# A scratch buffer laid out by chunk, and the last step's output norm moved off GpSimd

## The chip, the cores and the metric

The kernel runs on one core of a Trainium2 chip. The metric is the device time of one execution in microseconds. PE is TensorE (PEld its weight loads), DVE is VectorE, ACT is ScalarE, POOL is GpSimd, and SP is SyncE, which here only issues DMA transfers.

## What is computed

```python
def _gated_delta_rule(q, k, v, g, beta):
    ...
    def step(S, inp):
        q_t, k_t, v_t, g_t, b_t = inp
        S = S * jnp.exp(g_t)[..., None, None]
        mem = jnp.einsum('bhk,bhkv->bhv', k_t, S)
        delta = (v_t - mem) * b_t[..., None]
        S = S + jnp.einsum('bhk,bhv->bhkv', k_t, delta)
        o_t = jnp.einsum('bhk,bhkv->bhv', q_t, S)
        return (S, o_t)
...
o = _gated_delta_rule(q, k, v, g, beta)
o = o * jax.lax.rsqrt(jnp.mean(o * o, axis=-1, keepdims=True) + eps)
o = o * jax.nn.silu(g_out.reshape(Bm, Tm, H, DV))
attn = o.reshape(Bm, Tm, VAL_DIM) @ o_w.T
...
xn = _layernorm(x, axis=-1)
x = x + attn(xn) + ffn(xn)
```

x is (2, 4096, 512) in float32. The attention half has 16 heads with keys of 16 and values of 32; q, k and v come from a projection, a causal convolution of 4 taps and a SiLU. The feed-forward half has 1408 hidden columns with 4-bit weights and a final root-mean-square norm.

## The kernel before, in words

**Tiles.** The sequence is cut into 32 tiles of 128 positions, both batches (NB = 2) at once. The recurrence is done by chunks of 32 positions (CH = 32, NC = 4 chunks in a tile). Within a chunk it needs the inverse of a 32x32 unit triangular matrix for each batch, chunk and head: 2 x 4 x 16 = 128 matrices, one for each partition. GpSimd solves for them in `solve` (lines 478 to 499): 31 rounds of a product (line 495) and a subtraction (line 499), with matrix (b, c, h) in partition (b, c, h) and its 1024 elements in columns 1024 to 2048 of the tile `arena` (called `lt`).

**The turn through memory.** TensorE wants the same matrices the other way: row j of every head's matrix in partition c x 32 + j (the view `tT`, in columns 0 to 1024 of `arena`). SyncE does that with two kinds of transfer, at the end of its step. When the solve has signalled `t_done`, line 406 writes all 128 partitions, 4 KB each, to the scratch `scr_t`; line 408 waits until that has landed; line 412 then reads it back in eight transfers, one for each batch and chunk, each of 32 partitions x 16 heads x 128 bytes. On TensorE `t_times_r` (lines 1190 to 1205) waits for all eight, for the keys (`rk_done`) and for `out_done`, and then runs 256 small products (line 1202) in four groups. The other scratch, `scr_a`, does the opposite turn before the solve (lines 388 and 394).

**Order of the work.** Each engine runs its own hand-written step for a pair (t, n): the second half of tile t (recurrence, norm, output projection) beside the first half of tile n = t + 1 and n's feed-forward. `run` calls it once for the first tile, 30 times in a hardware loop, once for the last pair, and once with n absent: the last step, which has only the recurrence and the output of tile 31. On TensorE a step begins with `project(0)`, 16 products for the gates, `project(1)` to `project(4)`, and then `t_times_r(0)`, `project(5)`, `t_times_r(1)`, `t_times_r(2)`, `turn_qk(0)` and so on. Waits are in program order: whatever stands behind `t_times_r(0)` on TensorE waits with it. SyncE's next instructions after the reads are the loads of the next tile's x (line 384).

**The output norm.** In the last step, as in every step with a t, the output o is copied out of PSUM and squared by ScalarE (lines 754 and 759) and summed over each head's 32 values by VectorE (line 1032). GpSimd (`gated_and_scaled`, lines 513 to 527) multiplies o by the gate (line 517), forms mean plus eps (line 519), takes the power -0.5 (line 522) and scales o (line 527), for each batch. TensorE then turns o (`turn_o`, line 1347), ScalarE copies it (`o_columns`, line 667), TensorE multiplies by `wo` (line 1357), VectorE adds it to the result (line 912) and SyncE stores it (line 399).

**Other waits on the write.** `t_written` is also waited for by `solve` of the next tile (line 481) and by VectorE's `keep_rows(0)` (line 921), which overwrites the columns that the write reads.

Of the kernel before, what the change touches and what calls it, by code (L numbers as in the profile page):

```python
# [18 lines left out]
F32 = mybir.dt.float32  # L19
# [5 lines left out]
ALU = mybir.AluOpType  # L25
# [3 lines left out]
P = 128  # L29
NB = 2  # L30
# [61 lines left out]
def build(nc, A, out):  # L92
    NIT = A["x"].shape[1] // P
    scr_a = nc.dram_tensor("scr_a", (NB, NC, CH, H, CH), F32).ap()
    scr_t = nc.dram_tensor("scr_t", (NB, NC, H, CH, CH), F32).ap()

    with ExitStack() as ctx:
# [30 lines left out]
        negA = sb("negA", [P, H])  # L128
        eps = sb("eps", [P, 1])
        mhalf = sb("mhalf", [P, NB, H])  # L130

# [71 lines left out]
        a_read = signal("a_read", 128)  # L203
        t_written = signal("t_written", 16)
        t_read = signal("t_read", 128)

# [172 lines left out]
        def sp_step(eng, t, n, more):  # L379
            if more:  # L380
                m = n.next()
                hold(eng, *x_turned.at(n, NB))
                for b in range(NB):
                    eng.dma_start(xt[:, b, :], A["x"][b, bass.ds(m.number * P, P), :]).then_inc(x_loaded.sem, 16)
            if n:
                for b in range(NB):
                    hold(eng, *a_done.at(n, b + 1))
                    eng.dma_start(scr_a[b].rearrange("c j h i -> (c j) (h i)"), kbq[:, b, :]).then_inc(a_written.sem, 16)
                    hold(eng, *a_written.at(n, 16 * (b + 1)))
                    if b == 0:  # L390
                        hold(eng, *gram_out.at(n, NB))
                    for c in range(NC):
                        p0 = (b * NC + c) * H
                        eng.dma_start(la[p0:p0 + H, :, :],
                                      scr_a[b, c].rearrange("j h i -> h j i")).then_inc(a_read.sem, 16)
            if t:
                for b in range(NB):
                    hold(eng, *attn_added.at(t, b + 1))
                    eng.dma_start(out[b, bass.ds(t.number * P, P), :], obuf[:, b, :]).then_inc(out_stored.sem, 16)
                hold(eng, *out_stored.at(t, 16 * NB))  # L400
            if not n:
                return
            for b in range(NB):
                eng.dma_start(obuf[:, b, :], A["x"][b, bass.ds(n.number * P, P), :]).then_inc(res_loaded.sem, 16)
            hold(eng, *t_done.at(n, 1))
            eng.dma_start(scr_t[:, :, :, :, :].rearrange("b c h j i -> (b c h) (j i)"),
                          arena[:, 1024:2048]).then_inc(t_written.sem, 16)
            hold(eng, *t_written.at(n, 16))
            for b in range(NB):
                for c in range(NC):  # L410
                    s = slice(c * CH, (c + 1) * CH)
                    eng.dma_start(tT[s, b, :, :], scr_t[b, c].rearrange("h j i -> j h i")).then_inc(t_read.sem, 16)

# [64 lines left out]
        def solve(eng, n):  # L478

            if not n.first:  # L480
                hold(eng, *t_written.at(n.before(), 16))
            hold(eng, *qk_done.at(n, NB))
# [46 lines left out]
        def pool_step(eng, t, n, more):  # L529
            if n:  # L530
# [7 lines left out]
                keys_for_state(eng, t, n)  # L538
            if t:
                gated_and_scaled(eng, t)  # L540
# [28 lines left out]
        def act_step(eng, t, n, more):  # L569
# [92 lines left out]
            def o_columns():  # L662
                if not t:
                    return
                for b in range(NB):
                    eng.wait_ge(*o_turned.at(t, b + 1))
                    eng.activation(oT[b].rearrange("p k t -> p (k t)"), PS[:, 6 + b, :],
                                   ACT.Copy).then_inc(ot_copied.sem, 1)

            def y_rows():  # L670
                if not t:
# [65 lines left out]
            u_rows(1)  # L737
            decay(1)
            u_rows(2)
            masked_keys(0)  # L740
# [19 lines left out]
            unit(3)  # L760
            eng.preload_act_table_set(SILU)
            if n:
                gate(0)
                eng.wait_ge(*taps_done.at(n, NQKV))
# [8 lines left out]
                gate(2)  # L773
            if not n:
                o_columns()
                return
# [23 lines left out]
        def _(eng):  # L800
# [8 lines left out]
            eng.preload_act_table_set(EXP)  # L809
            eng.wait_ge(zeroed.sem, 4)  # L810
            first = Tile(0, 0, first=True)
# [36 lines left out]
        def dve_step(eng, t, n, more):  # L848
# [65 lines left out]
            def keep_rows(b):  # L914
# [5 lines left out]
                if t and b == 0:  # L920
                    eng.wait_ge(*t_written.at(t, 16))
                eng.tensor_copy(qk_rows[:, b, :], PS[:, 6 + b, :]).then_inc(qk_kept.sem, 1)
# [114 lines left out]
            hidden(1)  # L1037
            if not n:
                result(0)
                result(1)  # L1040
                return
# [16 lines left out]
        def _(eng):  # L1058
            eng.memset(eps[:, :], 1e-6).then_inc(zeroed.sem, 1)
            eng.memset(mhalf[:, :, :], -0.5).then_inc(zeroed.sem, 1)  # L1060
            eng.memset(halo[:, :, :, :], 0.0).then_inc(zeroed.sem, 1)
            eng.memset(S[:, :, :, :, :], 0.0).then_inc(zeroed.sem, 1)
            first = Tile(0, 0, first=True)
# [31 lines left out]
        def pe_step(eng, t, n, more):  # L1095
# [94 lines left out]
            def t_times_r(q):  # L1190
                if not t:
                    return
                if q == 0:
                    hold(eng, *rk_done.at(t, NB))
                    hold(eng, *t_read.at(t, 16 * NB * NC))
                    hold(eng, *out_done.at(t, NB))
# [274 lines left out]
        def _(eng):  # L1471
            eng.wait_ge(first_loaded.sem, 16 * 2)
            eng.wait_ge(zeroed.sem, 4)
            transpose_x(eng, Tile(0, 0, first=True), None)
# [66 lines left out]
```

## Time and profile before

| | before |
|---|---|
| median of 3 runs | 3350.01 us (3347.69 to 3350.68) |
| time of the profiled execution | 3347.2 us |
| its span | 3345.4 us |
| mean granted clock of TensorE | 0.988 of full speed |
| PE busy | 3174.2 us (95%) |
| DVE busy | 2429.0 us (73%) |
| POOL busy | 1840.9 us (55%) |
| ACT busy | 1664.4 us (50%) |

The span goes from the first to the last record of the profiled execution; the execution's own time is 1.8 us longer. An engine's busy time counts instructions, not the waits between them. A DMA's row in a timeline is the time in which SP issues it, not the time in which the data moves; that is seen in the DMA share (mean busy share of the core's 16 DMA engines) and GB/s of a window. Idle time in square brackets stands before a row, with what ended it.

### The profile page before, as it was taken

The numbers are of one execution on the slowest core, as the hardware profiler recorded it, in microseconds if no ns is written. First come the engines' busy times: TensorE is split into PE (matmuls) and PEld (weight loads), VectorE is DVE, ScalarE is ACT, GpSimd is POOL, SyncE is SP. The second block draws the span as 40 slices with busy tenths as digits, with TensorE's granted clock in tenths as the row PEclk, the third lists the DMA queues.
The fourth block names the chain that finished last, engine by engine and source line by source line (L and its number), as shares of the span: only waits on it lengthen the run. The fifth ranks groups of instructions, "written<-read, shape, count | busy, mean of one in ns | idle before, by whom it ended". The sixth has DMA issues, their size and how long they took to land.

```text
span 3345.4 us, 118358 instructions
## 1 busy us (share of the span) xinstructions
PE 3174.2 (95%) x45632; PEld 2253.2 (67%) x45632; DVE 2429.0 (73%) x5407; ACT 1664.4 (50%) x3306; POOL 1840.9 (55%) x2737
## 2 busy tenths in 40 slices
PE   5999999999999999999999999999999999999995
PEld 4666766766666766666666667666667666666664
DVE  7677777777777777777777777777777777777772
ACT  3444554545554445545445545445545455544452
POOL 3565455665455664456654456654556654466543
PEclk8999999999999999999999999999999999999996
DMA  3111111111111111111111111111111111111111
GB/s 111 39 46 27 37 43 33 45 39 27 40 40 39 46 33 30 43 34 45 46 27 37 43 33 46 45 26 35 43 36 46 36 28 43 37 42 46 27 31 30
DMA packets 318316, 132.07 MB, mean 39 GB/s; under 512 B 277088, under 2 KB 278880, under 8 KB 317792
## 3 DMA queue, kind: packets, MB, share of 16 engines
q1 hardware_dynamic: 313824, 119.26, 14.2%
q8 instruction: 383, 6.28, 0.8%
q10 hardware_dynamic: 4096, 6.42, 0.6%
q14 instruction: 13, 0.11, 0.0%
HBM read 75.30 MB, written 50.33 MB: 38 GB/s over the span
## 4 chain that ended last, share of the span: by engine, by line
PE 63%; DVE 13%; POOL 8%; issue 8%; ACT 4%; DMA 2%; SPq 1%; ACTq 1%; DVEq 1%; POOLq 0%
PE PS L1148 14%; PE PS L1216 7%; PE PS L1135 7%; PE PS L1104 6%; PE PS L1136 6%; PE PS L1357 5%; DVE arena L876 4%; POOL arena L499 4%; POOL work L495 3%; PE PS L1281 3%; PE PS L1202 3%; DVE inner L978 2%; PE PS L1234 2%; DVE arena L373 2%; PE PS L1252 2%
## 5 line engine op out<-in xcount | busy, mean ns | idle before, releaser
L876 DVE SCALAR_TENSOR_TENSOR arena<-PS,sc,arena 128x256 f32<-128x256 f32 x2112 | 1004.3, 482 | 294.0 <-ACT arena L596 193.6
L1135 PE MATMUL PS<-xh,wgu 128*128 128x256 f32 x2816 | 871.5, 341 | 36.0 <-DVE arena L876 35.5
L596 ACT ACTIVATE arena<-PS,sc 128x256 f32<-128x256 f32 x704 | 330.7, 475 | 759.6 <-PE PS L1136 703.6
L1136 PE MATMUL PS<-xl,wgu 128*128 128x256 f32 x2816 | 698.8, 281 | 0.0
L1148 PE MATMUL PS<-wdn,inner 128*128 128x512 f32 x1408 | 650.7, 592 | 0.0
L1135 PEld LDWEIGHTS PS<-xh,wgu 128*128 128x128 f32 x2816 | 531.2, 189 | 156.1 <-issue 85.2
L495 POOL TENSOR_TENSOR work<-arena 128x31 f32<-128x31 f32 (+15 forms) x992 | 511.4, 516 | 138.4 <-DMA arena<-scr_a 63.2
L499 POOL TENSOR_TENSOR arena<-arena,work 128x31 f32<-128x31 f32 (+15 forms) x992 | 543.7, 548 | 77.8
L1136 PEld LDWEIGHTS PS<-xl,wgu 128*128 128x128 f32 x2816 | 530.3, 188 | 83.2 <-issue 83.2
L1104 PE MATMUL PS<-xnT,wqkv 128*128 128x256 f32 x2048 | 498.7, 392 | 27.4 <-ACT inner L576 19.6
L1104 PEld LDWEIGHTS PS<-xnT,wqkv 128*128 128x128 f32 x2048 | 384.5, 194 | 107.5 <-ACT inner L576 33.2
L860 DVE SCALAR_TENSOR_TENSOR qkv<-inner,cw,qkv 128x256 f32<-128x256 f32 x768 | 419.6, 583 | 19.8 <-ACT qkv L583 10.6
L1148 PEld LDWEIGHTS PS<-wdn,inner 128*128 128x128 f32 x1408 | 245.6, 189 | 199.8 <-issue 199.3
L373 POOL TENSOR_TENSOR R<-arena,ckg 128x256 f32<-128x256 f32 x64 | 57.2, 912 | 399.9 <-DVE ckt L942 399.9
L1216 PE MATMUL PS<-wg,xnT 128*128 128x512 f32 x512 | 263.4, 618 | 0.1
L1357 PE MATMUL PS<-wo,arena 128*128 128x512 f32 x512 | 241.2, 594 | 0.0
L615 ACT ACTIVATE ub<-PS 32x512 f32<-32x512 f32 x256 | 136.8, 580 | 198.1 <-PE PS L1234 194.6
L517 POOL TENSOR_TENSOR arena<-arena 128x512 f32<-128x512 f32 x64 | 80.5, 1280 | 272.5 <-ACT qkv L759 272.5
L898 DVE TENSOR_TENSOR tmp<-PS,bdmask 128x128 f32<-128x128 f32 x256 | 74.2, 290 | 209.5 <-PE PS L1252 205.1
L888 DVE TENSOR_TENSOR inner<-arena,sg 128x256 f32<-128x256 f32 x352 | 203.6, 586 | 30.1
L607 ACT ACTIVATE sg<-arena 128x256 f32<-128x256 f32 x352 | 145.2, 412 | 153.9 <-DVE arena L876 153.5
L1054 DVE SCALAR_TENSOR_TENSOR obuf<-PS,yr,obuf 128x512 f32<-128x512 f32 x64 | 45.1, 746 | 217.8 <-POOL yr L511 217.8
(141 smaller groups left out, 4553.8 us busy)
## 6 DMA issues: line engine op xcount, KB each, us to landing
xt<-in_x SPq DMA_DIRECT2D x64, 256.0 KB, 2.8
scr_a<-arena SPq DMA_DIRECT2D x64, 256.0 KB, 2.4
arena<-scr_a SPq DMA_DIRECT2D x256, 64.0 KB, 3.2
obuf<-in_x SPq DMA_DIRECT2D x64, 256.0 KB, 2.8
scr_t<-arena SPq DMA_DIRECT2D x32, 512.0 KB, 2.7
arena<-scr_t SPq DMA_DIRECT2D x256, 64.0 KB, 2.3
out<-obuf SPq DMA_DIRECT2D x64, 256.0 KB, 2.0
wqkv<-in_wqkv ACTq DMA_DIRECT2D x1, 2048.0 KB, 12.9
```

The costliest lines, as they stand in the source:

```text
L495: eng.tensor_tensor(pr, la[:, j, j + 1:].unsqueeze(1).broadcast_to([P, w, r]), bc(lt[:, 0:w, j], r), ALU.mult).then_inc(solve_part.sem, 1)
L499: eng.tensor_tensor(tail, tail, pr, ALU.subtract).then_inc((t_done if j == CH - 2 else solve_part).sem, 1)
L596: eng.activation(fa[:, u % 4, :], PS[:, bank(u, 0), 0:NB * P], ACT.Copy, scale=sc[:, u % 2, KB * m:KB * m + 1]).then_inc(fa_scaled.sem, 1)
L860: eng.scalar_tensor_tensor(out=acc, in0=cin[:, mm, :, k:k + P], scalar=cw[:, mm, k:k + 1], in1=acc, op0=ALU.mult, op1=ALU.add).then_inc((t ...
L876: eng.scalar_tensor_tensor(out=fa[:, u % 4, :], in0=PS[:, bank(u, k // 2), k % 2 * NB * P:][:, 0:NB * P], scalar=sc[:, u % 2, KB * m + k:K ...
L888: eng.tensor_tensor(inner[:, m, :], fa[:, (2 * m + 1) % 4, :], sg[:, m % 2, :], ALU.mult).then_inc(h_done.sem, 1)
L1104: ins = eng.matmul(PS[:, proj_bank(m), 0:NB * P], wqkv[:, kb, m * P:(m + 1) * P], xnT[:, kb, :], start=(kb == 0), stop=(kb == KB - 1))
L1135: eng.matmul(o, w, xh[:, k, :], start=True, stop=False)
L1136: ins = eng.matmul(o, w, xl[:, k, :], start=False, stop=True)
L1148: ins = eng.matmul(PS[:, b, :], inner[:, m, b * P:(b + 1) * P], wdn[:, m, :], start=(m == 0), stop=(m == FM - 1))
L1216: ins = eng.matmul(PS[:, 4 + b, :], xnT[:, kb, b * P:(b + 1) * P], wg[:, kb, :], start=(kb == 0), stop=(kb == KB - 1))
L1357: ins = eng.matmul(PS[:, 6 + b, :], oT[b][:, kb, :], wo[:, kb, :], start=(kb == 0), stop=(kb == KB - 1))
```

## The change

There are two parts. The scratch `scr_t` is laid out with the chunk outermost, so that for one chunk both batches lie together. The write becomes two transfers, one for each batch, each from 64 partitions to 4 chunks x 16 heads; the read becomes four transfers, one for each chunk, each of 32 partitions x 32 (batch, head) x 128 bytes. The bytes are the same. The counts that others wait for follow.

In the last step alone, GpSimd no longer gates and scales the output: VectorE multiplies by the gate and by the scale, and ScalarE makes the scale as exp(-0.5 ln(mean + eps)) in `last_roots`, with a table load between the two. The load of the logarithm's table stands earlier in that step, between `u_rows(1)` and `u_rows(2)`, and the load of the SiLU table is left out there. The new eps tile is set once at the start, by one more memset that TensorE and ScalarE wait for with the others.

```diff
-    scr_t = nc.dram_tensor("scr_t", (NB, NC, H, CH, CH), F32).ap()
+    scr_t = nc.dram_tensor("scr_t", (NC, NB, H, CH, CH), F32).ap()
...
-        t_written = signal("t_written", 16)
-        t_read = signal("t_read", 128)
+        t_written = signal("t_written", 32)
+        t_read = signal("t_read", 64)
...
             hold(eng, *t_done.at(n, 1))
-            eng.dma_start(scr_t[:, :, :, :, :].rearrange("b c h j i -> (b c h) (j i)"),
-                          arena[:, 1024:2048]).then_inc(t_written.sem, 16)
-            hold(eng, *t_written.at(n, 16))
             for b in range(NB):
-                for c in range(NC):
-                    s = slice(c * CH, (c + 1) * CH)
-                    eng.dma_start(tT[s, b, :, :], scr_t[b, c].rearrange("h j i -> j h i")).then_inc(t_read.sem, 16)
+                eng.dma_start(scr_t[:, b].rearrange("c h j i -> c h (j i)"),
+                              arena[b * NC * H:(b + 1) * NC * H, 1024:2048]).then_inc(t_written.sem, 16)
+            hold(eng, *t_written.at(n, 16 * NB))
+            for c in range(NC):
+                s = slice(c * CH, (c + 1) * CH)
+                eng.dma_start(tT[s, :, :, :].rearrange("j b h i -> j (b h) i"),
+                              scr_t[c].rearrange("b h j i -> j (b h) i")).then_inc(t_read.sem, 16)
...
                 keys_for_state(eng, t, n)
-            if t:
+            if t and n:
                 gated_and_scaled(eng, t)
...
+            def last_roots():
+
+                eng.wait_ge(*so_done.at(t, NB))
+                eng.activation(ro[:, :, :], so[:, :, :], ACT.Ln, scale=1.0 / DV, bias=epso[:, :]).then_inc(ro_done.sem, 1)
+                eng.preload_act_table_set(EXP)
+                eng.wait_ge(*ro_done.at(t, 1))
+                eng.activation(ro[:, :, :], ro[:, :, :], ACT.Exp, scale=-0.5).then_inc(ro_done.sem, 1)
...
             decay(1)
+            if not n:
+                eng.preload_act_table_set(LOG)
             u_rows(2)
...
             unit(3)
-            eng.preload_act_table_set(SILU)
             if n:
+                eng.preload_act_table_set(SILU)
...
             if not n:
+                last_roots()
                 o_columns()
...
             if not n:
+                for b in range(NB):
+                    eng.wait_ge(*gs_done.at(t, 1))
+                    eng.tensor_tensor(sq[:, b, :], sq[:, b, :], gs[:, b, :], ALU.mult).then_inc(o_gated.sem, 1)
+                for b in range(NB):
+                    eng.wait_ge(*ro_done.at(t, 2))
+                    eng.wait_ge(*o_gated.at(t, b + 1))
+                    oh = sq[:, b, :].rearrange("p (h v) -> p h v", v=DV)
+                    eng.tensor_tensor(oh, oh, bc(ro[:, b, :], DV), ALU.mult).then_inc(o_scaled.sem, 1)
                 result(0)
                 result(1)
                 return
...
-                    hold(eng, *t_read.at(t, 16 * NB * NC))
+                    hold(eng, *t_read.at(t, 16 * NC))
```

## Rows read from the trace of the kernel before

**Rows 1.** The profile's page: busy time of the engines, and the chain that ended last.

```profile
PE 3174.2 (95%) x45632; PEld 2253.2 (67%) x45632; DVE 2429.0 (73%) x5407; ACT 1664.4 (50%) x3306; POOL 1840.9 (55%) x2737
...
PE 63%; DVE 13%; POOL 8%; issue 8%; ACT 4%; DMA 2%; SPq 1%; ACTq 1%; DVEq 1%; POOLq 0%
```

**Rows 2.** All matrix products on the triangles (line 1202): count, first and last start; transfer waits.

```profile
L1202 PE MATMUL PS<-R,arena x8192: 201/201/283, 145.4 to 3293.6; 32*32 32x48 f32 x200
...
  DMA arena<-scr_t: 9.8, 1
```

**Rows 3.** Timeline of SP's queue at one tile boundary: start us, us, engine, line.

```profile
1657.16 0.33 SPq L406 DMA_DIRECT2D scr_t<-arena  x1
1659.91 4.05 SPq L412 DMA_DIRECT2D arena<-scr_t  x8
```

**Rows 4.** The same boundary in windows: last columns PE's clock, DMA share, GB/s.

```profile
1657.98:1658.50 0.52, 0.52 (x6) 0.47 (x4) 0.00 (x0) 0.52 (x1) 0.41 (x1) 1.00 1.06 433
1658.50:1659.00 0.50, 0.50 (x8) 0.50 (x6) 0.10 (x1) 0.49 (x2) 0.48 (x2) 1.00 0.96 393
1659.00:1659.42 0.42, 0.42 (x6) 0.42 (x5) 0.42 (x1) 0.22 (x1) 0.42 (x1) 1.00 0.61 244
...
1661.50:1662.50 1.00, 1.00 (x6) 0.89 (x5) 1.00 (x2) 0.04 (x1) 0.88 (x1) 1.00 0.71 112
1662.50:1663.50 1.00, 1.00 (x6) 0.88 (x5) 0.92 (x4) 0.97 (x3) 0.00 (x0) 1.00 0.84 131
```

**Rows 5.** Timeline of PE at the same boundary.

```profile
1667.60 0.88 PE L1202 MATMUL PS<-R,arena 32*32 32x48 f32 x64
```

**Rows 6.** SP's queue, the next tile boundary.

```profile
1758.94 0.33 SPq L406 DMA_DIRECT2D scr_t<-arena  x1
```

**Rows 7.** Timeline of PE there.

```profile
1768.94 0.88 PE L1202 MATMUL PS<-R,arena 32*32 32x48 f32 x64
```

**Rows 8.** One tile's period in one window.

```profile
1667.60:1768.94 101.34, 98.43 (x1427) 69.92 (x1427) 74.59 (x170) 51.53 (x104) 57.04 (x86) 1.00 0.15 37
```

**Rows 9.** SP's queue in the last two steps.

```profile
3279.51 0.33 SPq L406 DMA_DIRECT2D scr_t<-arena  x1
3282.24 4.05 SPq L412 DMA_DIRECT2D arena<-scr_t  x8
```

**Rows 10.** Timeline of PE there.

```profile
3288.27 4.50 PE L1202 MATMUL PS<-R,arena 32*32 32x48 f32 x240 [9.79 <-DMA arena<-scr_t]
```

**Rows 11.** SP's queue: four reads of the other scratch, scr_a.

```profile
1614.23 1.90 SPq L394 DMA_DIRECT2D arena<-scr_a  x4
```

**Rows 12.** Windows from 1.7 us after these four reads began to be issued.

```profile
1615.91:1616.91 1.00, 1.00 (x4) 0.46 (x3) 0.90 (x3) 0.00 (x0) 1.00 (x1) 1.00 0.79 127
...
1618.41:1618.91 0.50, 0.50 (x7) 0.50 (x7) 0.47 (x2) 0.33 (x1) 0.00 (x0) 1.00 0.04 5
```

**Rows 13.** The last step's end: POOL.

```profile
3322.42 2.48 POOL L517 TENSOR_TENSOR arena<-arena 128x512 f32<-128x512 f32 x2 [41.82 <-ACT qkv L759]
...
3325.39 5.42 POOL L522 TENSOR_TENSOR ro<-ro,mhalf 128x32 f32<-128x32 f32 x1 [0.18 <-POOL ro L519]
3330.89 2.05 POOL L527 TENSOR_TENSOR arena<-arena,ro 128x512 f32<-128x512 f32 x2
```

**Rows 14.** The last step's end: DVE.

```profile
3322.44 1.28 DVE L1032 TENSOR_REDUCE so<-qkv 128x16 f32<-128x512 f32 x2 [7.31 <-ACT qkv L759]
3338.82 0.69 DVE L912 TENSOR_TENSOR obuf<-obuf,PS 128x512 f32<-128x512 f32 x1 [15.10 <-PE PS L1357]
```

**Rows 15.** The last step's end: ACT.

```profile
3322.88 1.28 ACT L761 ACT_TABLE_LOAD   x1
```

**Rows 16.** The last step's end: PE.

```profile
3331.99 2.12 PE L1347 MATMUL PS<-ident,arena 128*128 128x128 f32 x8 [11.30 <-POOL arena L527]
```

**Rows 17.** ACT in a middle tile: a logarithm of 128x32.

```profile
1666.08 0.21 ACT L705 ACTIVATE lnz<-ee 128x32 f32<-128x32 f32 x1
```

**Rows 18.** ACT in the last step, where the new table load is put.

```profile
3306.99 1.07 ACT L615 ACTIVATE ub<-PS 32x512 f32<-32x512 f32 x2 [3.42 <-PE PS L1234]
```

More of the change, by code:

```diff
@@ L129, in build @@
         eps = sb("eps", [P, 1])
+        epso = sb("epso", [P, 1])
         mhalf = sb("mhalf", [P, NB, H])
@@ L480, in solve @@
             if not n.first:
-                hold(eng, *t_written.at(n.before(), 16))
+                hold(eng, *t_written.at(n.before(), 16 * NB))
             hold(eng, *qk_done.at(n, NB))
@@ L809, in _ @@
             eng.preload_act_table_set(EXP)
-            eng.wait_ge(zeroed.sem, 4)
+            eng.wait_ge(zeroed.sem, 5)
             first = Tile(0, 0, first=True)
@@ L920, in keep_rows @@
                 if t and b == 0:
-                    eng.wait_ge(*t_written.at(t, 16))
+                    eng.wait_ge(*t_written.at(t, 16 * NB))
                 eng.tensor_copy(qk_rows[:, b, :], PS[:, 6 + b, :]).then_inc(qk_kept.sem, 1)
@@ L1061, in _ @@
             eng.memset(halo[:, :, :, :], 0.0).then_inc(zeroed.sem, 1)
+            eng.memset(epso[:, :], float(np.finfo(np.float32).eps)).then_inc(zeroed.sem, 1)
             eng.memset(S[:, :, :, :, :], 0.0).then_inc(zeroed.sem, 1)
@@ L1472, in _ @@
             eng.wait_ge(first_loaded.sem, 16 * 2)
-            eng.wait_ge(zeroed.sem, 4)
+            eng.wait_ge(zeroed.sem, 5)
             transpose_x(eng, Tile(0, 0, first=True), None)
```

## Prediction

> **What bounds the kernel.** I read the page first. TensorE is busy 95% of the span, and the chain that ended last runs on it for 63%, with VectorE and GpSimd far behind [rows 1]. So a stall that holds TensorE's queue in every tile costs its whole length, and a saving on a DMA queue is worth something only where TensorE waits for it. Next come the instructions that use what the changed transfers bring. The products on the triangles run from 145.4 to 3293.6 us, and only one of their 32 visits waits for the reads, for 9.8 us: the last [rows 2]. In the other 31 the turn through memory is hidden.
>
> How well it is hidden decides this case. At a middle boundary the write is issued at 1657.16 and the first read at 1659.91, 2.75 us later [rows 3]; TensorE comes to the products at 1667.60, or 10.44 us after the write was issued [rows 5]. One tile later the same distance is 1768.94 - 1758.94 = 10.00 us [rows 6, 7]. I take the mean, 10.2 us, as the time that the turn may take. What it does take is seen where nothing else is in the way, in the last step: write at 3279.51, reads from 3282.24, TensorE at 3288.27 [rows 9, 10]. That is 2.73 + 6.03 = 8.76 us. The cover is thus 10.2 - 8.8 = 1.4 us. Anything that makes the turn longer by more than 1.4 us is paid once a tile, and anything that makes it shorter is paid back once, in the last step.
>
> **The write.** In the trace the write's data are three windows: 0.52 x 433 + 0.50 x 393 + 0.42 x 244 = 524 KB [rows 4]. At a DMA share of 0.96 they move 393 GB/s, so 16 engines fully used move some 409 GB/s and the data need 1.28 us. The rest of the 2.75 us, 1.47 us, is issue, start and landing. The new write is two transfers whose destination leads with 4 chunks, each of 16 rows; the old one led with 128 rows. The trace has no transfer that leads with fewer than 16 rows, so it does not show how many engines share such a one. I bound it from both sides. If all 16 share it, the data still need 1.28 us, and the second issue (0.33 us, like the first [rows 3]) is hidden behind the first one's data: plus 0.0 to 0.4 us. If the leading rows are what is dealt out, 4 engines get everything, at 409 / 4 = 102 GB/s: 524 / 102 = 5.13 us, or plus 3.85 us. Both writes would go to the same 4, since the second is dealt out like the first. Fewer than 4 is not plausible, as 4 leading rows and 64 partitions both divide by 4. I take the long end: the leading dimension is the one that both sides of every transfer in this kernel could always be dealt by, and 4 is all that it now has. From write to first read: 1.47 + 5.13 = 6.60 us.
>
> The Trainium skill states a rule for this, in "DMA: Bandwidth & Descriptors", section "Why a DMA increments its semaphore by 16 and not by 1": a transfer uses the largest count of engines, up to 16, that divides the slowest dimension of both its sides. By it the count here is 4, and the sum would be the one below. No row of this trace shows it.
>
> **The reads.** Eight issues take 4.05 us [rows 3, 9]; four would take some 2.0 us. If the reads went at the pace at which they are issued, 2.0 us would be saved. But the data move at 112 to 131 GB/s with a DMA share of 0.71 to 0.84 [rows 4], and the packets stay 128 bytes: 524 KB at 121 GB/s are 4.3 us, longer than the issues of even the old form. So the pace is mostly that of the packets. Were the share to rise from 0.78 to 1, the same packets would need 3.4 us and 0.9 us would be saved. The other side is the reads of the other scratch. Four issued in 1.90 us [rows 11], with the same small packets, still move data in the window that ends 4.7 us after their first issue, at a share of 0.04, while up to 2.7 us it was 0.79 [rows 12]: once the issues run ahead, a few engines straggle. 4 x 64 KB at 121 GB/s are 2.2 us of data, so the stragglers stretch a batch by some 1.5 us (an estimate, from 4.7 less 2.2 and less about 1 us of start). Between a gain of 2.0 and a loss of 1.5 us I take a gain of 0.3 us, near the data rate of the row.
>
> The Trainium skill's "DMA: Bandwidth & Descriptors", section "Rules for kernel authors", advises to coalesce small transfers, since under 64 KB one pays mostly overhead. The old reads are 64 KB each. By that rule alone the gain would be near the 2.0 us of the issues; the data rate in the rows speaks against it.
>
> **The sum for a middle tile.** New turn: 6.60 + 6.03 - 0.3 = 12.3 us, against 10.2 us at which TensorE arrives: it stalls 2.1 us. Behind the wait in its queue stand project(5), the other product groups, turn_qk and all of the recurrence; ScalarE and VectorE wait for these in turn, so nothing downstream goes on without them. In a whole tile of 101.34 us TensorE is idle for 2.9 us [rows 8], in short pieces, so there is little to swallow a stall. GpSimd's next solve starts from what TensorE makes later, so it shifts by the same amount and the next boundary looks alike. The first boundary has more cover: its products start at 145.4 [rows 2]. That leaves 30 tiles: 30 x 2.1 = +63 us. The x loads behind the reads on SP are issued some 2 us later, and their data are used over 10 us later: nothing. The later `t_written` waits of VectorE and GpSimd are passed well before they are reached: nothing.
>
> **The last step.** The turn is uncovered: 12.3 - 8.8 = +3.6 us. Then the norm. Before, GpSimd gates from 3322.42 for 2.48 us, takes the power from 3325.39 for 5.42 us, and scales from 3330.89; TensorE starts at 3331.99 [rows 13, 16]. After: the sums start at 3322.44, 0.64 us each [rows 14], done by about 3323.8. ScalarE's logarithm takes 0.21 us [rows 17], the table load 1.28 us [rows 15], the exponential 0.21 us as its like, and the handovers some 0.4 us: 3325.9. VectorE's scaling of one batch I price at 0.65 us, by the addition of the same size that takes 0.69 us [rows 14]; its two gatings (1.3 us) fit between 3323.8 and 3325.9. TensorE starts at about 3326.5: -5.5 us. The logarithm's table is loaded in a wait of 3.42 us [rows 18], so it costs nothing; without that cover it would cost 1.28 us. The extra memset is one small instruction before the input has landed: nothing. Last step: 3.6 - 5.5 = -1.9 us.
>
> **Total.** The profiled execution's own 3347.2 + 63 - 1.9 = 3408.3 us; its time stands 2.8 us below the median of the runs. I predict 3408 us.
>
> **Rivals.**
> (A, forecast, 0.74) Four engines; a stall of 1.4 to 3.2 us a tile. Its own range is 3386 to 3442 us.
> (B, 0.13) All 16 engines share the writes. The turn then takes at most 8.8 + 0.4 us, below 10.2; nothing in the loop changes, and the norm alone pays. 3350 - 5.5 - 0.3 = 3344 us. For it: every transfer in the trace reaches a share near 1 or is bound by packets. Against: none leads with so few rows. It decides as soon as the write's data need less than 1.28 + 1.4 = 2.7 us. This is the one that ends on the faster side.
> (C, 0.07) Four engines, but the reads are bound by their issues: a gain of 1.0 to 2.0 us, and a stall of 0.4 to 1.4 us. 3347 + 12 to 42 + up to 2 - 5.5: 3355 to 3385 us.
> (D, 0.06) Four engines, and the reads straggle as scr_a's do, 1.5 us later than before: a stall of 2.1 + 0.3 + 1.5 = 3.9 us. 3347 + 117 + 5.4 - 5.5 = 3464 us.
>
> **Range and chances.** 3352 to 3442 us holds A and C and leaves out B and D, some 2 in 10. About 0.2% (6.7 us) is what a measurement of this kernel can tell from no change. Below 3343.3 us lies about half of B: 0.06. Within 0.2% the rest of B and a little of C: 0.09. Slower: 0.85.
>
> **What would show it.** In the trace after: the distance from the first write to the first read (6.6 us by A, 2.8 to 3.2 us by B); the DMA share while the write runs (near 0.25 over 5 us, or near 1 over 1.3 us); the time from first read to last landing; the products on the triangles waiting for a DMA in some 30 tiles, about 2 us each; the distance from write to products (12.3 us); and in the last step TensorE's turn_o some 5.5 us earlier behind the squares. I am wrong if the write's windows show a share near 1, or if the waits are there and the tile's period is not longer than 101.3 us.

## The result, and the profile after

The changed kernel takes 3588.34 us (median of 4 runs, 3587.82 to 3590.29) against 3350.35 us, a ratio of 1.071 (95% interval 1.070 to 1.073). Slower was forecast; the size was not: 3408 us, range 3352 to 3442. The profiled span grew by 243.0 us, from 3345.4 to 3588.4 us. Where a kernel ran more than once, its time and ratio here and below are of its fast runs; an execution in a slower state, as one of e1_rows64 at 4911.6 us, is left out.

On the page, the shares of busy time and the chain that ended last answer to [rows 1]:

```profile
PE 3239.1 (90%) x45632; PEld 2302.4 (64%) x45632; DVE 2419.8 (67%) x5412; ACT 1668.3 (46%) x3309; POOL 1836.7 (51%) x2731
...
PE 31%; POOL 30%; DMA 19%; issue 6%; DVE 6%; SPq 5%; POOLq 2%; ACT 1%; ACTq 0%; DVEq 0%
POOL arena L501 15%; POOL work L497 14%; DMA scr_t<-arena 8%; PE PS L1238 7%; PE PS L1126 6%; DMA scr_a<-arena 4%; DMA arena<-scr_t 4%; PE PS L1224 3%; DMA arena<-scr_a 3%; PE PS L1303 3%; SPq L395 3%; PE PS L1256 2%; PE PS L1274 2%; DVE arena L374 1%; SPq L413 1%
```

TensorE's share of the chain fell from 63% to 31%. GpSimd's solve (line 501 is 499 of before, and line 497 is 495), DMA and the scratch buffers took its place: the turn through memory has become part of the loop that sets the time. In the waits (who waited, on what, us in total, times, longest), TensorE's products on the triangles, line 1224 now, wait for the reads on all 32 visits, where before only the last one did [rows 2]:

```profile
PE PS L1224 <- DMA arena<-scr_t: 192.1, 32, 16.8
```

One boundary shows where this comes from. SP's queue and TensorE, as in [rows 3, 5]:

```profile
1772.42 1.14 SPq L408 DMA_DIRECT2D scr_t<-arena  x2
1782.37 2.15 SPq L413 DMA_DIRECT2D arena<-scr_t  x4
```

```profile
1788.35 1.50 PE L1224 MATMUL PS<-R,arena 32*32 32x48 f32 x64 [5.37 <-DMA arena<-scr_t]
1789.78 3.78 PE L1126 MATMUL PS<-xnT,wqkv 128*128 128x256 f32 x8
...
1795.03 0.66 PE L1182 MATMUL PS<-ident,qkv 128*128 128x128 f32 x4
```

First read 9.95 us after the first write (before 2.75, forecast 6.60). TensorE is at the products 15.93 us after the write (before 10.44 and 10.00, forecast 12.3); from first read to products it takes 5.98 us (forecast 5.73). The first product after the stall and project(5) behind it are slow as well: 3.78 us for eight products that took 1.99 us in other places. The windows tell both (columns: window, length, busy time of PE, PEld, DVE, ACT and POOL with counts, TensorE's clock, DMA share, GB/s):

```profile
1774.00:1776.00 2.00, 2.00 (x17) 1.95 (x17) 1.80 (x3) 0.50 (x2) 1.80 (x3) 1.00 0.23 43
1776.00:1778.00 2.00, 2.00 (x11) 1.77 (x10) 1.97 (x3) 0.24 (x1) 1.68 (x1) 1.00 0.25 70
1778.00:1780.00 2.00, 2.00 (x11) 1.74 (x11) 1.60 (x5) 1.95 (x5) 0.00 (x0) 1.00 0.24 94
1780.00:1782.00 2.00, 1.80 (x9) 1.27 (x8) 1.78 (x8) 1.92 (x6) 0.00 (x0) 1.00 0.11 43
...
1788.35:1790.35 2.00, 2.00 (x65) 1.81 (x66) 0.00 (x0) 0.00 (x0) 0.00 (x0) 0.50 0.08 24
1794.00:1796.00 2.00, 2.00 (x144) 1.77 (x135) 0.00 (x0) 0.79 (x2) 0.00 (x0) 1.00 0.04 8
```

While the writes run, the DMA share is 0.23 to 0.25: four engines of sixteen. But they move 43, then 70, then 94 GB/s, and not the 102 GB/s that four should. They do not end together either: from 1780 to 1782 the share is 0.11, on average fewer than two engines, and the reads wait for the last of them. And when TensorE starts again after 5.4 us of idling, its granted clock is 0.5 (1.2 GHz) and comes back to 1.0 by 1794.

The period of the loop, from the first writes' first and last starts. The instructions of the tile `scr_t` (duration min, median, max, first and last start):

```profile
L408 SPq DMA_DIRECT2D scr_t<-arena x64: 507/523/666, 133.2 to 3521.9; - x64
```

The last step's first write is at 3521.36, so a tile takes (3521.36 - 133.2) / 31 = 109.3 us, against (3279.51 - 133.2) / 31 = 101.5 us before: +7.8 us, 242 of the 243 us. One tile in one window, here from one first write to the next:

```profile
1772.42:1882.19 109.77, 101.26 (x1430) 71.93 (x1429) 74.59 (x168) 52.09 (x106) 57.10 (x85) 0.97 0.15 35
```

The rest is the last step, +7.0 us in the turn and -5.6 us in the norm. The turn, as [rows 9, 10]: 3537.09 - 3521.36 = 15.73 us, against 8.76.

```profile
3521.36 1.09 SPq L408 DMA_DIRECT2D scr_t<-arena  x2
3531.18 2.21 SPq L413 DMA_DIRECT2D arena<-scr_t  x4
```

```profile
3537.09 4.68 PE L1224 MATMUL PS<-R,arena 32*32 32x48 f32 x240 [16.82 <-DMA arena<-scr_t]
```

The norm, as [rows 13 to 16], on ScalarE, VectorE and TensorE:

```profile
3573.08 0.32 ACT L675 ACTIVATE ro<-so,epso 128x32 f32<-128x32 f32 x1 [0.90 <-DVE so L1045]
3573.42 1.28 ACT L676 ACT_TABLE_LOAD   x1
3574.71 0.23 ACT L678 ACTIVATE ro<-ro 128x32 f32<-128x32 f32 x1
```

```profile
3571.77 1.28 DVE L1045 TENSOR_REDUCE so<-qkv 128x16 f32<-128x512 f32 x2 [7.60 <-ACT qkv L771]
...
3574.97 1.29 DVE L1059 TENSOR_TENSOR arena<-arena,ro 128x512 f32<-128x512 f32 x2 [0.73 <-ACT ro L678]
```

```profile
3575.72 1.97 PE L1369 MATMUL PS<-ident,arena 128*128 128x128 f32 x8 [5.70 <-DVE arena L1059]
```

From the first sum to TensorE's turn_o it is 3575.72 - 3571.77 = 3.95 us, against 3331.99 - 3322.44 = 9.55 us: 5.6 us less.

### The profile page after: what moved, and what is told of

Read it like the earlier page. It is cut to its first block, busy times and chain, and to the rows that moved or that the text cites. A ratio compares the mean times of both kernels' runs of the same rounds, so it can differ in the third digit from the quotient of the medians.

```text
span 3588.4 us, 118230 instructions
## 1 busy us (share of the span) xinstructions
PE 3239.1 (90%) x45632; PEld 2302.4 (64%) x45632; DVE 2419.8 (67%) x5412; ACT 1668.3 (46%) x3309; POOL 1836.7 (51%) x2731
## 4 chain that ended last, share of the span: by engine, by line
PE 31%; POOL 30%; DMA 19%; issue 6%; DVE 6%; SPq 5%; POOLq 2%; ACT 1%; ACTq 0%; DVEq 0%
POOL arena L501 15%; POOL work L497 14%; DMA scr_t<-arena 8%; PE PS L1238 7%; PE PS L1126 6%; DMA scr_a<-arena 4%; DMA arena<-scr_t 4%; PE PS L1224 3%; DMA arena<-scr_a 3%; PE PS L1303 3%; SPq L395 3%; PE PS L1256 2%; PE PS L1274 2%; DVE arena L374 1%; SPq L413 1%
## 5 line engine op out<-in xcount | busy, mean ns | idle before, releaser
L1126 PE MATMUL PS<-xnT,wqkv 128*128 128x256 f32 x2048 | 546.4, 420 | 27.6 <-ACT inner L578 19.2
L1126 PEld LDWEIGHTS PS<-xnT,wqkv 128*128 128x128 f32 x2048 | 416.0, 210 | 120.0 <-ACT inner L578 32.2
L1224 PE MATMUL PS<-R,arena 32*32 32x48 f32 x8192 | 129.2, 224 | 192.8 <-DMA arena<-scr_t 192.1
L1224 PEld LDWEIGHTS PS<-R,arena 32*32 32x32 f32 x8192 | 115.7, 122 | 226.5 <-issue 226.5
L935 DVE COPY arena<-PS 128x512 f32<-128x512 f32 x64 | 44.0, 687 | 309.6 <-ACT arena L635 300.0
```

Of the source, the lines that this page charges most:

```text
L1126: ins = eng.matmul(PS[:, proj_bank(m), 0:NB * P], wqkv[:, kb, m * P:(m + 1) * P], xnT[:, kb, :], start=(kb == 0), stop=(kb == KB - 1))
L1224: ins = eng.matmul(x_rows(c, r)[:, 0:3, (b * NHALF + f) * 2 + e, :], tT[s, b, h, :], R[s, b, h, :], start=(b + f + e == 0), stop=False, sk ...
```

## The experiments

Line numbers are those of each kernel. "First read" is the time from the first write's issue to the first read's, "products" that from the first write's issue to TensorE's start on them, both at a boundary in the middle. All use the changed kernel as the base unless something else is said. In the second column [4 x 16] stands for 4 leading rows of 16 each; the count of engines is read from the DMA share. One packet of a write is one row of 4 KB; at the rate of the write before (409 GB/s on 16 engines) an engine needs 0.16 us for it. What the runs on the write gave:

| run | what it writes | engines | first read, us | time, us | ratio to before |
|---|---|---|---|---|---|
| before | 1 x 128 rows | 16 | 2.75 | | 1 |
| changed | 2 x [4 x 16] | 4 | 9.95 | 3588.3 | 1.071 |
| e1_rows64 | 2 x 64 | 16 | 3.85 | 3338.5 | 0.998 (0.997 to 0.999) |
| e3_lead8 | 2 x [8 x 8] | 8 | 5.74 | 3368.4 | 1.008 (1.006 to 1.009) |
| e2_pad | 2 x [4 x 16], 132 KB apart | 4 | 10.04 | 3577.0 | 1.069 (1.067 to 1.070) |
| e12_onelead4 | 1 x [4 x 32] | 4 | 10.19 | 3593.0 | 1.074 (1.072 to 1.076) |
| e6_serial | 2 x [4 x 16], one at a time | 4 | 11.16 | 3605.5 | one run |
| e14_rows | 2 x [4 x 16], side by side | 4 | 9.94 | 3574.8 | one run |
| e13_alt4 | 2 x [4 x 16], even and odd partitions | 4 | 8.49 | 3523.0 | one run |
| e15_quarters | 4 x [4 x 8] | 4 | 7.24 | 3454.4 | one run |

**e1_rows64: the same two writes and four reads, but 64 rows lead.** The scratch's rows are ordered chunk, head, batch, so that a batch's 64 rows have one stride.

```diff
-scr_t (NC, NB, H, CH, CH);  write scr_t[:, b] "c h j i -> c h (j i)"
+scr_t (NC, H, NB, CH, CH);  write scr_t[:, :, b] "c h j i -> (c h) (j i)"
-tT = arena[:, 0:1024] "p (b h i) -> p b h i"
+tT = arena[:, 0:1024] "p (h b i) -> p b h i"
```

> The changed kernel, but each of the two writes leads with 64 rows (rows of the scratch ordered chunk, head, batch), and the four reads stay. Theory 1 (the leading dimension of a transfer sets how many engines share it): first read some 2.9 us after the first write instead of 9.95, a turn of 8.9 us, hidden again below the 10.2 us of cover; the loop is as before and the last step keeps its gain: about 3345 us. Theory 2 (two writes and four reads of twice the size are slow by themselves, whatever leads): near the 3588 us of the changed kernel.

SP's queue in it:

```profile
1656.61 1.12 SPq L408 DMA_DIRECT2D scr_t<-arena  x2
1660.46 2.44 SPq L413 DMA_DIRECT2D arena<-scr_t  x4
```

3338.5 us, ratio 0.998 (0.997 to 0.999), and 3.85 us to the first read instead of 2.9. Theory 1 holds: with two writes and four reads as in the changed kernel the whole of the 238 us is gone, so what leads in the write made it slower.

**e3_lead8: eight leading rows.** Rows in the order chunk, half, batch, eight heads.

```diff
+scr_t (NC * 2, NB, H // 2, CH, CH);  write scr_t[:, b] "c h j i -> c h (j i)"
+tT = arena[:, 0:1024] "p (e b g i) -> p b e g i"
```

> The changed kernel, with writes that lead with 8 (chunk and half of the heads) x 8 rows; same four reads. If the leading dimension sets the engines, 8 sem packets a write, and a DMA share of 0.5 at most. Theory B of e2 with time going as one over the engines: data 4.15 us, first read after 5.8 us, turn 11.8 us, a stall of 1.6 us without a fall of TensorE's clock: 3345 + 48 + 3 = 3396 us. With the old packet rate on 8 engines, 2.6 us of data, turn 10.2 us: 3345 to 3350 us. If the count of engines is not the cause: 3588 us.

```profile
1665.90 1.27 SPq L408 DMA_DIRECT2D scr_t<-arena  x2
1671.64 2.30 SPq L413 DMA_DIRECT2D arena<-scr_t  x4
```

```profile
1668.90:1669.90 1.00, 1.00 (x7) 0.90 (x7) 1.00 (x2) 0.00 (x0) 1.00 (x1) 1.00 0.49 156
```

1.008 (1.006 to 1.009), with a stall of 1 us a tile (41.5 us in 31 waits, 12.4 of them in the last step); the first read comes where theory B put it (5.8 us), the time below its 3396 us. With 64, 8 and 4 leading rows the first read comes after 3.85, 5.74 and 9.95 us. Less the 1.47 us of issue and landing these are 2.4, 4.3 and 8.5 us, close to one over the number of engines (38, 34 and 34 when multiplied by it). With the share, 0.49 here for eight engines and 0.23 to 0.25 for four, that settles the count. What it leaves open is the rate: at 0.16 us a packet, the 128 packets need 20 us summed over the engines and not 34.

**e2_pad: four engines, 132 KB apart in memory.**

```diff
+scr_t (NC, NB * H + 1, CH, CH);  write scr_t[:, b*H:(b+1)*H]; read scr_t[c, 0:NB*H]
```

> The changed kernel, with one unused row behind each chunk in the scratch, so that the four leading rows of a write lie 132 KB apart and not 128 KB. The writes still lead with 4. Theory A (addresses 128 KB apart get in each other's way and make the write take 8.3 us of data where four engines at the old packet rate need 5.1): first read after about 6.7 us, a turn of 12.7 us, 3345 + 30 x 2.5 + 4 = about 3424 us. Theory B (four engines are slow for another reason): as the changed kernel, 9.9 us and 3588 us.

First read after 10.04 us, ratio 1.069 (1.067 to 1.070): theory A falls.

**e4_norm: the last step's norm alone**, on the kernel before.

> The kernel before with the new last-step norm alone. The prediction's term: 5.5 us less, 3344.9 us. The rival, that the table loads or the extra wait eat it: within 2 us of the kernel before.

3337.3 us against 3344.8 of the kernel before beside it, ratio 0.998 (0.997 to 0.999). The term of 5.5 us lies in the interval (3.7 to 9.7 us less).

**e5_twice: the kernel before, with its write done twice**, to measure the cover with a known delay.

```diff
 hold(eng, *t_written.at(n, 16))
+eng.dma_start(scr_t ..., arena[:, 1024:2048]).then_inc(t_written.sem, 16)
+hold(eng, *t_written.at(n, 32))
```

> The kernel before, with the same 128-row write done a second time after the first has landed: the turn is 2.75 us longer, 11.5 us, with nothing else changed. The prediction's cover of 1.4 us (10.2 less 8.8) and one for one passing: a stall of 1.3 to 1.4 us in 30 tiles and 2.75 us in the last step, +43 us. If the stall were taken up elsewhere in the tile: below +10 us.

The write is at 1789.17 and the products here:

```profile
1800.76 0.88 PE L1205 MATMUL PS<-R,arena 32*32 32x48 f32 x64 [1.60 <-DMA arena<-scr_t]
```

```profile
PE PS L1205 <- DMA arena<-scr_t: 55.1, 31, 12.7
```

The turn is 11.6 us and the stall 1.6 us here, 55.1 us in 31 waits. Less the last step's 12.7 us, that is 1.4 us a tile, as expected. The time rose by more, to a ratio of 1.017 (1.014 to 1.019), which is +48 to +63 us: so 1.4 us of stall cost some 1.8 us. Nothing in the tile takes a stall up; it costs a little more than itself. TensorE's rows show where: behind the stall it pauses in the same products for 14.5 us in 24 pauses, waiting for nothing that the profile shows; the kernel before has 1.0 us in 3 such pauses.

**e10_warm and e11_warm12: does the clock cost the rest?** Products of a projection into a free bank ahead of the wait keep TensorE busy through the stall (20 in the first, 12 in the second).

```diff
+if n:
+    for i in range(12):
+        eng.matmul(PS[:, 7, 0:NB * P], wqkv[:, i % KB, 0:P], xnT[:, i % KB, :], start=True, stop=True)
 hold(eng, *t_read.at(t, 16 * NC))
```

> The changed kernel, with 20 products of a projection (into a free bank, their result unused) ahead of the wait for the reads, 20 x 0.24 = 4.8 us of the 5.4 to 6.0 us that TensorE stands still there. If the clock at half speed after that idle time is what costs the 2.1 us a tile beyond the stall: the clock stays at 1.0, the period falls from 109.1 to about 107 us and the time to 3588 - 30 x 2.1 = 3525 us. If the clock has no part in it: 3588 us.

It went to 3644.1 us, ratio 1.090. The expectation had the price of a product wrong, as TensorE's rows show (the write is at 1799.52):

```profile
1809.51 8.80 PE L1219 MATMUL PS<-xnT,wqkv 128*128 128x256 f32 x40
1818.24 0.88 PE L1227 MATMUL PS<-R,arena 32*32 32x48 f32 x64
```

Each product is two records, and 20 take 8.80 us, so they hold TensorE until 18.7 us after the write. It tells nothing of the clock's price.

> As e10_warm, but with 12 products in place of 20: there each took 0.44 us and not 0.24 (8.8 us for the 20), so that they themselves held TensorE until 18.7 us after the write. 12 take 5.3 us and end before the reads land at 15.9 us. The clock stays at 1.0, the period falls from 109.1 to about 107 us and the time to 3588 - 30 x 2.1 = 3525 us. If the clock has no part in it: 3588 us.

The boundary with the write at 1770.66:

```profile
1786.35 0.88 PE L1227 MATMUL PS<-R,arena 32*32 32x48 f32 x64 [0.36 <-DMA arena<-scr_t]
1787.16 1.99 PE L1126 MATMUL PS<-xnT,wqkv 128*128 128x256 f32 x8
...
1793.25 0.36 PE L1227 MATMUL PS<-R,arena 32*32 32x48 f32 x13 [1.31 <-issue]
```

The stall is 0.36 us, project(5) takes 1.99 us again and not 3.78: the clock stays up here. turn_qk(0) comes 4.2 us after the first product (1790.58 - 1786.35), against 6.7 us in the changed kernel (1795.03 - 1788.35). In the kernel before it takes 4.4 us (1672.04 - 1667.60). So the fall of the clock costs over 2 us at the boundary. The whole run's granted clock is 0.985 here and 0.960 in the changed kernel. But the time is 3573.5 us and not 3525, only 14.8 us or 0.5 us a tile less than the changed kernel: in the last group of small products TensorE now stops for 1.31 us, waiting for nothing that the profile shows ("issue"). Over the run this is 45.8 us in 43 pauses, or 1.5 us a tile, of the kind that e5_twice has too; the changed kernel, at the slower clock, has one, of 0.7 us. What they are stays open. So the clock's price is shown at the boundary and not in the total: what the kernel would gain from a clock that stays up lies between the 0.5 us a tile that e11 got and the 2.2 us of the boundary.

**e6_serial: one write at a time.**

```diff
 eng.dma_start(scr_t[:, b] ..., arena[b * NC * H:(b + 1) * NC * H, 1024:2048])
+hold(eng, *t_written.at(n, 16 * (b + 1)))
```

> The changed kernel, with a wait between its two writes, so that only one is on its way at a time. Theory C (the two writes hinder each other on the four engines): each takes 1.47 + 16 packets x 0.16 = 4.0 us, the first read comes after 8.1 us instead of 9.95, and the time falls by some 30 x 1.9 = 55 us. Theory D (a write that only four engines share is slow by itself at 4.15 us of data): first read after 11.3 us or more, and 3588 + 30 x 1.4 = about 3630 us.

```profile
1781.81 6.13 SPq L408 DMA_DIRECT2D scr_t<-arena  x2
1792.97 2.21 SPq L413 DMA_DIRECT2D arena<-scr_t  x4
```

11.16 us to the first read, so some 5.6 us for each write and 4.1 us of data (5.6 - 1.47) for 16 packets an engine: theory D, though the time rose less than it foretold (3605.5 us against about 3630). The two writes do not hinder each other.

**e12_onelead4: one write, still four engines.** The solve's matrices stand in partition order chunk, batch, head (as in e9_onewrite, below), the scratch has one unused row behind each chunk.

> As e9_onewrite (one write of all 128 partitions, four reads), but the write leads with 4 (chunks of 32 rows, one unused row behind each). It tells the count of engines from the split in two. At the packet time of the 16-engine write (0.16 us): 32 packets are 5.1 us, first read after 6.6 us, turn 12.5 us, stall 2.3 us, 3337 + 30 x 2.3 + 4 = 3410 us. At the 0.26 us a packet that the changed kernel's writes need on average: 8.3 us, first read after 9.8 us, about 3580 us.

```profile
1772.97 0.59 SPq L407 DMA_DIRECT2D scr_t<-arena  x1
1783.16 2.42 SPq L412 DMA_DIRECT2D arena<-scr_t  x4
```

10.19 us, ratio 1.074 (1.072 to 1.076): the split in two is not the cause either. e9_onewrite, below, writes the same rows of the same partitions at once and differs in the unused row alone, so that its write leads with 128 rows: 3344.7 us against 3593.0.

**e7_halves and e8_evenodd: the kernel before, its write in two, 16 engines each**, once by lower and upper half of the partitions and once by even and odd ones.

```diff
+for b in range(NB):    # e7
+    eng.dma_start(scr_t[b] "c h j i -> (c h) (j i)", arena[b * 64:(b + 1) * 64, 1024:2048])
+for b in range(NB):    # e8
+    eng.dma_start(scr_t "b c h j i -> (b c h) (j i)"[b:P:2], arena[b:P:2, 1024:2048])
```

> The kernel before, with the write split into two of 64 rows, each to one contiguous half of the scratch; 16 engines share each. e1_rows64 took 2.2 us of data for the same bytes (first read after 3.85 us) where the one write takes 1.4 (2.75 us). If its scattered rows were the cause: 1.4 us and a first read after some 3.0 us here. If it is that each transfer reads only half of the partitions: 2.2 us and 3.85 us again. The time stays with the kernel before either way, within 0.1%, since both are below the 10.2 us of cover.

> The kernel before, with the write split into two of 64 rows, one of the even and one of the odd partitions. In e7_halves, with the lower and the upper half of the partitions, the first read came after 3.83 us where the one write has 2.75. If that is because each transfer reads from one half of the partitions only: about 3.1 us here (2.75 and one more issue). If it is two transfers as such: 3.83 us again. The time stays with the kernel before.

e7, its queue and the window in which the writes' data move:

```profile
1758.70 1.12 SPq L407 DMA_DIRECT2D scr_t<-arena  x2
1762.53 4.05 SPq L413 DMA_DIRECT2D arena<-scr_t  x8
```

```profile
1759.83:1762.00 2.17, 2.17 (x19) 2.09 (x19) 1.92 (x3) 0.54 (x2) 1.98 (x3) 1.00 0.94 242
```

e8, the same:

```profile
1757.14 1.13 SPq L407 DMA_DIRECT2D scr_t<-arena  x2
1760.23 4.06 SPq L413 DMA_DIRECT2D arena<-scr_t  x8
```

```profile
1758.29:1759.73 1.44, 1.44 (x15) 1.44 (x15) 1.26 (x2) 0.48 (x2) 1.25 (x3) 1.00 0.91 361
```

The same bytes, engines and number of transfers: 242 GB/s from one half of the partitions, 361 GB/s from every second one, with the DMA share above 0.9 in both, and 3.83 against 3.09 us to the first read. In e8 the rows of each write also alternate in memory, but so do those of e1_rows64, which reads halves and has 3.85 us. So the partitions that a transfer reads set its speed here. The times: e8 3345.7 us (one run), e7 1.002 (1.001 to 1.003), which is 0.2% more than expected and not explained; none of its reads is waited for before the last step.

**e13_alt4, e14_rows: source or destination?** e13 puts batch 0 into the even and batch 1 into the odd partitions. e14 lets the four engines write side by side in memory.

```diff
-arena[b * NC * H:(b + 1) * NC * H, 1024:2048]
+arena[b:P:NB, 1024:2048]                        # e13
-scr_t (NC, NB, H, CH, CH)
+scr_t (NB, H, NC, CH, CH)                       # e14
```

> The changed kernel, with batch 0 in the even and batch 1 in the odd partitions (the reads of scr_a land there), so that each write still leads with 4 x 16 rows on four engines, but takes its rows from all 128 partitions, and each engine's 16 from 32 partitions. At 16 engines this made the split write as fast as it can be (e8_evenodd). If reading from few partitions is also what keeps the four engines at 0.26 us a packet: data 5.1 us, first read after 6.7 us, 3345 + 30 x 2.5 = about 3420 us. If not: first read after 9.9 us and 3588 us.

> The changed kernel, with the scratch's rows in the order batch, head, chunk: each write still leads with 4 chunks x 16 rows on four engines, but the four write side by side (rows 4 KB apart, each engine's next row 16 KB on) and not 128 KB apart. e2_pad moved them only to 132 KB. If where the four engines write in memory is what slows them: first read clearly before 9.9 us, down to 6.7 us. If not: 9.9 us and 3588 us; the reads, of 128 bytes every 16 KB, may change by some tenths.

e13's queue:

```profile
1743.47 1.18 SPq L408 DMA_DIRECT2D scr_t<-arena  x2
1751.96 2.32 SPq L413 DMA_DIRECT2D arena<-scr_t  x4
```

```profile
1745.47:1746.47 1.00, 1.00 (x9) 0.97 (x9) 1.00 (x3) 0.00 (x0) 0.82 (x2) 1.00 0.08 16
...
1747.47:1748.47 1.00, 1.00 (x7) 0.87 (x6) 1.00 (x2) 0.08 (x1) 0.83 (x1) 1.00 0.27 111
```

e13 takes 1.5 us off the first read, between its two forecasts; e14, at 9.94 us, nothing. Where the rows go has no part in it, where they come from has. In e13 nearly the whole loss is at the start: the third microsecond after the issue moves 16 GB/s, and from the fifth on the four engines run at the full 111 GB/s.

**e15_quarters: four engines that read elsewhere.** If the leading rows are dealt out in order, engine k reads partitions 16k to 16k + 15 of its half in the changed kernel, so that engines 0 and 2, and 1 and 3, are 32 partitions apart as long as they keep step. Here they are 8, 16 and 24 apart. (The matrices land under other heads and chunks, so this kernel does not compute the right result; its transfers are of the same sizes.)

```diff
-for b in range(NB): write scr_t[:, b] from arena[b * 64:(b + 1) * 64]
+for q in range(4):
+    h = slice(q % 2 * HG, (q % 2 + 1) * HG)
+    eng.dma_start(scr_t[:, q // 2, h] "c h j i -> c h (j i)", arena[q * 32:(q + 1) * 32, 1024:2048])
```

> The changed kernel, with the write in four transfers of 32 partitions, each leading with 4 groups of 8 rows (the matrices land in the scratch under other heads and chunks than they belong to, so the recurrence computes with misplaced triangles; the bytes, engines and packets are the same). Still four engines and 32 packets for each. What changes is which partitions the four engines read at the same time: 8 apart here, 16 apart in the changed kernel. Theory P (engines whose partitions are 32 apart share a way out of SBUF, as the halves of e7 against the even and odd rows of e8 suggest; here no two of the four are 32 apart): 32 packets at 0.16 us = 5.1 us of data, first read after 6.8 us, 3345 + 30 x 2.6 = about 3425 us. Theory Q (four engines are slow whatever they read): first read after 9.9 us or more, 3588 us or more.

```profile
1704.86 2.67 SPq L409 DMA_DIRECT2D scr_t<-arena  x4
1712.10 2.21 SPq L414 DMA_DIRECT2D arena<-scr_t  x4
```

```profile
1717.91 0.88 PE L1225 MATMUL PS<-R,arena 32*32 32x48 f32 x64 [2.35 <-DMA arena<-scr_t]
```

7.24 us to the first read, and 13.05 us to the products, with a stall of 2.35 us. The data need 7.24 - 1.47 = 5.8 us with four issues (2.67 us in all) among them, near the 5.1 us of the packets. Theory P foretold the first read within half a microsecond (6.8 us; its time, 3425 us, was 29 us short), and it accounts for 2.7 of the 3.3 us by which the forecast of the write was short. Two things keep it from being shown in full. The write is in four transfers here and not in two, and that alone was not tried (one against two makes no gain: 10.19 and 9.95 us). And e13's four engines are 32 partitions apart from one another as well, and still reach 111 GB/s once they are under way; that engines fall out of step there would explain it, but no run tested it.

The Trainium skill's "SBUF — State Buffer", section "Door 1: The DMA port swizzle (why `[64,N]` ≈ `[32,N]`)", says that bits 4 to 2 and bit 6 of a partition's number pick one of 16 ports, so that partitions 32 apart within a half share one and a half reaches only 8 ports. The traces agree in three places: the halves at 242 GB/s, the even rows at 361, and the four engines that are not 32 apart at nearly the full packet rate. By the same rule e13's engines share ports two by two as those of the changed kernel do, and there the 111 GB/s are not explained by it.

**e9_onewrite: chunk order in the partitions, one write, four reads.**

```diff
-p0 = (b * NC + c) * H
+p0 = (c * NB + b) * H
+eng.dma_start(scr_t "c b h j i -> (c b h) (j i)", arena[:, 1024:2048])
```

> The changed kernel, with the solve's matrices in partition order chunk, batch, head (the reads of scr_a land there), so that one write of 128 rows fills the scratch laid out by chunk, and the four reads stay: first read 2.75 us after the write, a turn of 2.75 + 5.9 = 8.7 us. The loop as before, the last step as in e4_norm or 0.1 us better: a ratio of 0.998 to the kernel before. If four reads of twice the size were worth the 2.0 us of their issues, the last step would begin its products 6.8 us after the write.

The last step:

```profile
3278.51 0.33 SPq L407 DMA_DIRECT2D scr_t<-arena  x1
3281.25 2.14 SPq L412 DMA_DIRECT2D arena<-scr_t  x4
```

```profile
3286.93 3.34 PE L1223 MATMUL PS<-R,arena 32*32 32x48 f32 x155 [9.55 <-DMA arena<-scr_t]
```

Ratio 1.000 (0.999 to 1.001), 3344.7 us in that comparison. The turn of the last step is 3286.93 - 3278.51 = 8.42 us, 0.3 us less than before. This is the four reads' whole worth: 3286.93 - 3281.25 = 5.68 us from first read to products, against 6.03. The loop's cover of 10.2 us hides even that. e9's last step has the same norm as e4, so a ratio like e4's 0.998 was due; the two intervals just touch, and no run sets them side by side. The versions that measured clearly below the kernel before are e4_norm (3337.3 us) and e1_rows64 (3338.5 us), by 0.2%. Both have the new norm, and it is the only part of the change with a gain that shows in the time.

## Why the prediction was wrong

**What held.** The turn was hidden by a cover of 1.4 us: e5_twice measured it. The leading dimension deals out the engines: a share of 0.25, and e1 and e3. The reads gained 0.3 us when measured alone (forecast 0.3); the rival of 2.0 us fell. TensorE swallows none of a stall. The norm: -5.6 us (forecast -5.5). The rule that the prediction cites for the count of engines agrees with the trace: a share of 0.25 with 4 leading rows, of 0.49 with 8.

**Where it failed: the write's term.** "If the leading rows are what is dealt out, 4 engines get everything, at 409 / 4 = 102 GB/s: 524 / 102 = 5.13 us." The count was right, the rate was not. The rate of a 16-engine transfer was divided by four as if each engine carried its own rate wherever it reads. It took 9.95 us to the first read in place of 6.60, +3.3 us: the data need 8.5 us and not 5.13. That this hangs on the partitions that the four engines read is shown (e13, e15; e2 and e14 rule out the place in memory); that it is engines 32 partitions apart slowing each other down is the reading that fits e15_quarters (7.24 us), e3 and e7 against e8, with e13's later stretch unexplained. And the 5.13 us stood as the upper bound: the range had nothing beyond.

**A term that was not in the sum: the clock.** The forecast's stall of 2.1 us was priced as itself. At 5.4 us and more TensorE's clock fell to 1.2 GHz in every tile, and the stretch from the first product to turn_qk(0) grew by some 2 us (6.7 us, against 4.4 before and 4.2 in e11). At the boundary shown the stall of 1.6 us in e5_twice left it at 1.0, and the run's clock is 0.988 as before. In e15_quarters, with stalls of 2.8 us a tile, it is 0.977 against 0.989: so a stall near the 2.1 us of the forecast may already bring it down in some tiles.

**The sum again.** Products at 15.9 us instead of 10.2: +5.7 us a tile. Behind them +2.1 us, the length of what the clock costs at the boundary (2.2 us over before); but e11, which kept the clock up, got back only 0.5 us of it. Together +7.8 us, as measured; times 31 is 242 us (the first boundary, whose 12.2 us of cover I had let pass, is stalled too), and the last step adds 7.0 - 5.6. The forecast's 2.1 us a tile was short by 3.3 (write), 0.3 (reads: 5.98 us from first read to products against 5.73) and 2.1 (behind the stall, where it had nothing).

**The rivals.** B (16 engines) fell; it is what e1_rows64 brings about. C and D were about the reads, and neither came. The true outcome was none of the four: the range reached only as far as the mechanisms that I had named for the reads, while the doubtful number was the write's.

## What to carry to other kernels

The DMAs here were dealt out over the engines by their slowest dimension, so ask of every rearranged transfer what now leads on each side: writing "c h (j i)" for "(c h) (j i)" cost 7% here. Fewer issues are worth little where the data rate sets the pace (0.3 us of 6.0 here), and that only where somebody waits. When a hidden transfer may come out from its cover, price the wait beyond its length too, since TensorE came back at half its clock after 5.4 us; and set the range by the least known rate, not by the best known.

## What the runs showed of the hardware

- The rate of a write depends on the partitions that its engines read at the same time. Four engines took 8.5 to 8.7 us of data for 512 KB with sources 16 or 32 apart (changed kernel, e12), 7.0 us in e13 with every second partition, and 5.8 us with sources 8 apart (first read less 1.47 us). On 16 engines, 242 GB/s from 64 neighbouring partitions and 361 GB/s from 64 even ones.
- Where the rows go in memory did not matter: 4 KB, 128 KB or 132 KB between the engines gave 9.94, 9.95 and 10.04 us to the first read.
- An issue on SP of a write that leads with 4 x 32 rows takes 0.59 us (e12), one of 128 rows 0.33 us (e9).
- Four reads of 128 KB reached the products 5.68 us after the first issue, eight of 64 KB 6.03 us.
- After 5.4 us of waiting TensorE's clock was at 1.2 GHz for the first products of the tile, and back at 2.4 GHz 6 us later.
